# Last two layers of a four-layer GNN kernel: 2 of 26 parts gathered and 24 summed from the count matrix, in place of 6 and 20

## The reference, cut to what matters

```
src = concatenate([edge_index[0], loops]); dst = concatenate([edge_index[1], loops])
dis = rsqrt(deg); norm = dis[src] * dis[dst]
def _gcn_conv(x, W, b, src, dst, norm, n):
    h = x @ W.T
    msg = h[src] * norm[:, None]
    return segment_sum(msg, dst, num_segments=n) + b
h = relu(_gcn_conv(x, W1, b1, ...)); return _gcn_conv(h, W2, b2, ...)
```

## Time and profile before

| what | us |
|---|---|
| median of 3 runs | 3882.71 |
| span of the profiled execution | 4355.4 |
| layer 3, about 3603 to 3970 of that span | 367 |
| layer 4, about 3976 to 4341 | 365 |
| what follows the last piece | 15 |

### The profile page before, as it was taken

The page is one execution under the profiler, slowest core; times in us unless marked ns, Lnnn a source line. Parts: engine busy times, 40 slices in busy tenths (PEclk is TensorE's granted clock), DMA queues, the critical chain, the costliest instruction groups (busy, mean ns, idle before and its releaser), DMA issues. The chain is left out here.

```text
span 4355.4 us, 78937 instructions
## 1 busy us (share of the span) xinstructions
PE 3123.5 (72%) x19042; PEld 2324.3 (53%) x19043; DVE 2245.6 (52%) x6922; ACT 1982.0 (46%) x2698; POOL 2898.9 (67%) x2439
## 2 busy tenths in 40 slices
PE   4777877777777771565666666666888887887887
PEld 3444544444444440344444444445777777887877
DVE  7877777777777775344444444444022323223223
ACT  3555565555655553000001000103666666766665
POOL 3888888888888887666666666664655553553554
PEclk7888788887888885677777777777988998998898
DMA  8555666655655657111111111112444446766665
GB/s 283 99 101 101 108 112 111 106 103 104 116 101 98 108 102 246 44 47 47 48 51 49 48 48 51 49 48 71 128 137 139 138 136 186 217 212 200 203 198 155
DMA packets 362034, 506.40 MB, mean 116 GB/s; under 512 B 58808, under 2 KB 260748, under 8 KB 361324
## 3 DMA queue, kind: packets, MB, share of 16 engines
q0 software_dynamic: 178752, 183.65, 24.5%
q1 hardware_dynamic: 130122, 230.91, 17.6%
q10 hardware_dynamic: 52898, 89.11, 5.6%
HBM read 336.75 MB, written 170.10 MB: 116 GB/s over the span
## 5 line engine op out<-in xcount | busy, mean ns | idle before, releaser
L978 POOL DMA_INDIRECT rows<-t,idx_ring x1184 | 1141.7, 964 | 716.1 <-issue 329.3
L1686 PE MATMUL bank<-arena 128*128 128x384 bf16 (+1 forms) x2496 | 682.0, 409 | 397.5 <-DVE arena L2374 300.1
L1022 POOL DMA_INDIRECT sums<-rows,idx_ring x416 | 666.7, 1603 | 143.5 <-issue 115.1
L1022 POOL DMA_INDIRECT sums<-stage,idx_ring x416 | 667.2, 1604 | 126.9 <-issue 100.4
L1553 PE MATMUL bank<-planes,x_sides 128*128 128x256 f32 x3920 | 578.9, 302 | 72.2 <-issue 58.9
L978 POOL DMA_INDIRECT rows<-xp,idx_ring x384 | 373.3, 972 | 376.7 <-DMA xp<-alpha 114.3
L1553 PEld LDWEIGHTS bank<-planes,x_sides 128*128 128x128 f32 x3920 | 528.1, 204 | 84.5 <-issue 74.0
L1424 PE MATMUL bank<-S,rows 128*128 128x192 f32 x1664 | 514.4, 446 | 0.6 <-issue 0.6
L1121 ACT ACTIVATE node_data<-bank,most_sb 128x408 f32 x720 | 391.4, 602 | 229.5 <-PE bank L1689 201.5
L1686 PEld LDWEIGHTS bank<-arena 128*128 128x128 bf16 x2496 | 174.6, 109 | 599.6 <-issue 452.4
L2373 DVE TENSOR_SCALAR arena<-S 128x1176 bf16<-128x1176 int16 x832 | 450.0, 541 | 0.5 <-issue 0.5
(11 more groups left out here) (266 smaller groups left out, 5083.6 us busy)
## 6 DMA issues: line engine op xcount, KB each, us to landing
adj<-node_data ACTq DMA_DIRECT2D x112, 448.0 KB
rows<-adj SPq DMA_DIRECT2D x102, 448.0 KB
bases_sb<-adj SPq DMA_DIRECT2D x65, 448.0 KB
arena<-src SPq DMA_DIRECT2D x104, 256.0 KB
rows<-t,idx_ring POOLq DMA_INDIRECT x1184
adj_even<-node_data ACTq DMA_DIRECT2D x77, 224.0 KB
S<-adj SPq DMA_DIRECT2D x36, 448.0 KB
arena<-type SPq DMA_DIRECT2D x52, 256.0 KB
```

Source lines behind the costliest of these rows:

```text
L978: nc.gpsimd.indirect_dma_start(out=(part_rows if p > 2 else rows)[:, k, t, :], out_offset=None, in_=row_tables[p], in_offset=bass.Indirect ...
L1022: nc.gpsimd.indirect_dma_start(out=sums_t[t], out_offset=bass.IndirectOffsetOnAxis(ap=idx4[:, k, t:t + 1], axis=0), in_=msg[k][:, t, :], i ...
L1686: nc.tensor.matmul(bank[bk][:, 0:(hb - ha) * W], lo, hw_hot[n * GT + t][:, ha * W:hb * W], start=t == 0, stop=False)
```

## The change

One table is shorter: parts 5, 9, 17 and 21 of layers 3 and 4 are summed and no longer gathered. All of them are odd, so their pieces are typed.

```
-GATHER_PARTS = (5, 9, 13, 17, 21, 25)
+GATHER_PARTS = (13, 25)
 DENSE_PARTS = tuple(q for q in range(NPT) if q not in GATHER_PARTS)
 LPARTS, LCHUNKS = len(GATHER_PARTS), len(DENSE_PARTS)
 LPIECES, LGROUPS = LCHUNKS * NPC, LPARTS * GPH
```

## The result

The changed kernel takes 3955.91 us (median of 4 runs, 3953.68 to 3960.95), the kernel before in the same measurement 3880.65 us (4 runs, 3876.44 to 3882.92): ratio 1.0195, 95% interval [1.0182, 1.0207], so +75 us where +62 was forecast.

The account below looks back on a forecast made before the run. PE was taken to bound layers 3 and 4, with ACT close behind: +46.5 us for pieces, -15.4 for groups, so +31.1 a layer and +62.2 for both. Added to 3882.7 this gave 3944.9 us, range 3925 to 3962.

Parts of the forecast that it names:

- PE's price: Layers 3 and 4: 28 more pieces cost PE 46.5 us, 64 fewer groups save 15.4: +31.1 us a layer, +62.2 both.
- POOL's floor: Before the change, POOL's gathers could hold layers 3 and 4 to 279 and 269 us, making the price 51 us.
- ACT's share: Layers 3 and 4: ACT gets 44.5 us more a layer but stays behind PE, adding a few us or less.
- The margin of 6 and 11 us to PE: After the change ACT needs 300.9 us against PE's 307.4 in layer 3, 280.6 against 291.2 in layer 4.
- waits shrink by themselves: Argument against the rival on ACT: an engine that is behind finds its inputs ready, so its waits shrink.
- The sign that I had named for PE's pace: If PE counts, ACT's turned pieces wait for PE's buffers and lie 2 to 4 us ahead of it.
- The second rival: Layers 3 and 4: ACT with its waits becomes the engine that counts, +23 us more, +85 in all, 3968 us; chance 0.18.
- DMA: Bytes cancel per layer: 28 more pieces cost +40.8 us of 16 engines, 128 fewer gathers save 46.6; no bound.
- The first rival: Layers 3 and 4: PE's standing time goes with the gathers, -103 + 62 = -41 us, 3842 us; chance 0.13.
- the 472.7 us: Whole kernel: the profiled execution is this much longer than the median; most of PE's excess was held for the profile's own.
- the standing of 154 us: Layers 3 and 4: PE's time beyond its work after the gathers begin, 72 + 82 us, held mostly for the profile's own.
- The third rival: Loads of the pieces set the pace; bytes are the same, so no difference, 3883 us; chance 0.06.

Follow-up runs that it names:

- experiment 2: Kernel before, with ACT turning only the first half of each piece of layers 3 and 4 to fp32: 3869.97 us, ratio 0.9962.
- experiments 2 and 3: ACT turns only the first half of each piece of layers 3 and 4: in the kernel before 3869.97 us, then in the changed kernel 3925.21 us.
- Experiment 4: Kernel before, with one gather a group in place of two in layers 3 and 4, PE using its rows twice: 3879.36 us, ratio 0.9982.
- experiment 12: Kernel before, with all gathers of layers 3 and 4 fetching rows of 256 bytes in place of 768: 3881.14 us, ratio 0.9992.
- experiment 11: Kernel before, with one gather a group in place of two in layers 3 and 4, where the kernel before takes 4351.5 us: 4198.82 us, ratio 0.9651.

## Why the prediction was right, and where its reasons were wrong

**PE's price.** Forecast +31.1 us a layer; the layers grew by 36.7 and 37.9. The counts are as foreseen (2352 and 192 matmuls a layer), and so are the unit prices: in the timeline of PE above, five pieces and a group take 3700.20 - 3691.64 = 8.56 us, and 5 x 1.66 + 0.24 is 8.54. From experiment 2 to 3 PE's busy time grows by 62.0 us, the sum again; the two layers grow by 57.7, since PE's wait for gathers goes at the same time, a term that the forecast had only in the other end of its price (POOL's floor). That calm stretches of a disturbed profile gave the undisturbed prices was right: 11.62 us for seven pieces is from chip B and holds on A.

**ACT's share, the term that was mis-sized.** I took "a few us of ACT's or less", and experiments 2 and 3 give 17 to 20 us. The excess of the layers over 62.2 is only 12, since the gathers' 4 to 7 us went the other way: that these two partly cancel is luck. ACT's totals were right (300.9 and 280.6 us against 303.95 and 275.67 busy). The margin of 6 and 11 us to PE is by the busy times 14 and 27 (317.92 and 302.47 for PE), so wider than reckoned, and still it didn't cover the waits. What failed is the sentence that waits shrink by themselves in an engine that is behind: the wait for the moments, 2.82 us, is for DVE, which itself follows PE's turning, so it comes in every block and shrank only from 28.3 to 22.1 us in the 11 blocks of layer 4. The sign that I had named for PE's pace, ACT's pieces 2 to 4 us ahead, holds in layer 3 (median 2.9 us) and fails in layer 4 (0.9). The second rival had named this mechanism and priced it at 23 us for both layers; it gave 17 to 20. The waits that grew lie mostly in layer 4, where L1389 waits 11.7 of its 14.0 us. The time, 3955.91 us, lies between forecast and rival, inside the forecast's own range of 3925 to 3962.

**POOL's floor** of 279 and 269 us was the other end for PE's price (51 us, so 11 less). Experiment 4 prices the gathers at 7 us in the kernel before, and experiments 2 and 3 put the price without ACT at 55 to 58. So neither end was right by itself; the forecast's "between 51 and 62" was.

**DMA.** Queue q1 carries 63.07 MB in layer 3 (50.04 on chip A before), q0 6.30 (18.89): +13.0 and -12.6. After, then before on chip A:

```profile
q1 hardware_dynamic: 31154, 63.07, 59.5%
...
q0 software_dynamic: 3072, 6.30, 6.5%
```
```profile
q1 hardware_dynamic: 26765, 50.04, 50.7%
q0 software_dynamic: 9216, 18.89, 22.3%
```

Over windows of 340 and 302 us these are +49 us of 16 engines on q1 and -45 on q0, where +40.8 and -46.6 had been worked out. It cancels as foreseen, and experiment 12 says that in the kernel before even 12.6 MB less a layer hardly count.

**The first rival and the 472.7 us.** This is where the reasoning was wrong though the sign came out. I held the standing of 154 us for the profile's own, with two arguments. One was that the 472.7 us must be somewhere: they are another chip (profiled span 3885.7 on A and 4301.4 for the changed kernel on B, each within 0.3% of the same kernel's other runs there but the far one). The other was that layer 2 stands only 5.0 us for no visible cause. That was the idle time of one group. Windows over the whole of layer 2, chip B:

```profile
3010.00:3603.00 593.00, 501.73 (x2421) 416.07 (x2420) 154.00 (x536) 389.81 (x336) 338.82 (x352) 0.91 0.46 134
```

and chip A:

```profile
2805.00:3282.00 477.00, 460.25 (x2420) 386.83 (x2418) 152.62 (x535) 390.63 (x336) 340.05 (x352) 0.99 0.58 167
```

PE is idle for 91 us there and for 17 here, with the same matmuls: layer 2 loses 116 us on chip B. Most of the idle time there has the name of a wait for ACT or DVE and only some 20 us none, so a look at PE's own "issue" could not have found it. The excess was real, and 149 us of it lie in layers 3 and 4, close to the 154 of the prediction (about 4 us of which, in the first of the two windows behind the first gathers, are the wait for the table and no stall within a piece). Where it exists, the rival is right, and its size nearly: -55 us on chip B against its -41. Its share that goes with two thirds of the gathers is 86%, not two thirds. The chance of 0.13 was for the wrong question; the right one is on which chip the time is taken, and that it was one of A's kind was luck for the forecast. The third rival is excluded: the bytes are the same and the time is not.

## What to carry to other kernels

When a profile's span and the runs' times differ by 12%, suspect two machines before the profiler, and look for the same idle time in every stage, by windows and not by one group's row. A trade of one engine's work for another's should be tried with each of the two nearest engines relieved in turn: here PE's sum gave the size, and a block's wait that takes the lead of an engine only 0.07 us a piece faster gave the rest. Such a wait is cheaper to move by two slots than to pay (19 us on chip B).

## What the hardware showed unexpectedly

The same program takes 3881 to 3887 us by the medians of three measurements and 4350 to 4351 us on chip B, in 20 runs there; by the traces the difference is 205 us before layer 2, 116 in layer 2, 149 in layers 3 and 4, and nothing behind. Where experiment 11 halved the gathers of the last two layers, those two lost it entirely and the layers ahead of them kept it. That in these two layers the stalls of that chip come with the gathers is shown by what removes them. That close neighbours count for more than numbers is a correlation, whether rows or bytes count is open, and what the gathers share there with PE and ACT, which both stand, was not found. What makes the layers before them longer there was not tested.
